# A GNN edge network on one core: first keys evicted ahead of head 3's norm, the rectifier in eight pieces inside the chain, and GpSimd adding the halves of the squared outputs

## The reference

```python
scale = 1.0 / np.sqrt(2.0 * O)
q_i = K_v[dst]
alpha = concatenate([q_i * K_v[src], q_i * K_E], axis=1) * scale
gate = sigmoid(_ln(alpha, ln_g[h], ln_b[h]))
m = concatenate([V_v[src], V_E], axis=1)
m = (m @ Wu[h] + bu[h]) * gate
m = _leaky(_ln(m @ Wm[h] + bm[h], mln_g[h], mln_b[h]))
heads.append(segment_sum(m, dst, num_segments=n))
```

## Time and profile before

| what | value |
|---|---|
| median of 3 runs | 12,400.16 us (12,395.85 to 12,402.57) |
| the profiled execution's own time | 12,403.94 us |
| its span, first to last instruction | 12,402.1 us |
| mean granted TensorE clock | 0.978 |
| busy over the span: PE, DVE, ACT, POOL | 76%, 69%, 54%, 53% |
| edge network, first to last gate (L722) | 4,182 to 10,434 us |

### The profile page before, as it was taken

One profiled execution on the slowest core, in us unless ns is written; L12 is line 12 of the kernel. 1 busy time (PEld: TensorE's weight loads), 2 busy tenths in 40 slices (PEclk: granted clock), 3 DMA queues, 4 the chain that ended last, 5 costly groups with the idle time before them and its releaser, 6 DMA issues.

```text
span 12402.1 us, 195341 instructions
## 1 busy us (share of the span) xinstructions
PE 9426.5 (76%) x48422; PEld 6119.9 (49%) x48423; DVE 8554.8 (69%) x19173; ACT 6685.0 (54%) x13488; POOL 6548.5 (53%) x4199
## 2 busy tenths in 40 slices
PE   1344444444446799999999999999999997769996
PEld 1233333333322566666666666666666665333222
DVE  4233333333311799999999999999999998047896
ACT  0111111111100488888888888888888886026442
POOL 1588888888840366666666666666666664000000
PEclk9999999999999799999999999999999998989997
DMA  9866666666678455555555555555555553869663
GB/s 412 257 163 150 152 150 151 150 152 152 149 234 337 153 152 152 152 152 152 152 152 152 152 152 152 152 152 152 152 152 152 152 152 109 355 255 358 206 218 118
DMA packets 1446102, 2253.42 MB, mean 182 GB/s; under 512 B 352561, under 2 KB 981762, under 8 KB 1432131
## 3 DMA queue, kind: packets, MB, share of 16 engines
q1 hardware_dynamic: 1129144, 1975.67, 48.0%
q0 software_dynamic: 312672, 272.36, 13.6%
q10 hardware_dynamic: 4144, 3.51, 0.1%
HBM read 1758.01 MB, written 492.97 MB: 181 GB/s over the span
## 4 chain that ended last, share of the span: by engine, by line
PE 42%; POOL 15%; ACT 15%; issue 12%; DMA 8%; DVE 3%; SPq 3%; ACTq 1%; DVEq 0%; POOLq 0%; PEldq 0%
POOL adj L1473 14%; ACT arena L1014 8%; PE psum L1274 6%; PE psum L1259 6%; PE psum L1248 5%; PE psum L1345 5%; DMA arena<-adj 5%; PE psum L1240 4%; PE psum L1214 4%; SPq L1520 3%; ACT acc L1005 3%; DMA adj<-put_val,put_idx 3%; PE psum L1390 2%; PE psum L1266 2%; ACT arena L986 2%
## 5 line engine op out<-in xcount | busy, mean ns | idle before, releaser
L1473 POOL DMA_INDIRECT adj<-put_val,put_idx x1616 | 2640.7, 1634 | 842.6 <-issue 477.2
L1155 PE MATMUL psum<-ke,arena 64*128 64x256 f32 x3232 | 1451.8, 640 | 1883.2 <-DMA arena<-in_edge_t 1883.2
L1014 ACT ACTIVATE arena<-arena 128x128 f32<-128x128 f32 x6464 | 2624.5, 501 | 19.1 <-DVE arena L788 9.1
L1434 POOL DMA_INDIRECT arena<-table,idx_blk x1616 | 1938.1, 1199 | 451.3 <-issue 409.3
L1155 PEld LDWEIGHTS psum<-ke,arena 64*128 64x128 f32 x3232 | 1041.6, 330 | 2292.9 <-issue 2025.9
L971 ACT ACTIVATE arena<-psum 128x512 f32<-128x512 f32 x808 | 482.5, 597 | 2921.5 <-PE psum L1155 2611.7
L1486 POOL TENSOR_TENSOR arena<-arena,mg 128x1024 f32<-128x1024 f32 x404 | 953.6, 2360 | 1973.7 <-DVE arena L800 1973.7
L1248 PE MATMUL psum<-arena,wvu 128*128 128x512 f32 x3232 | 1655.3, 594 | 0.0
L1259 PE MATMUL psum<-wm,arena 128*128 128x64 f32 x12928 | 1616.3, 278 | 0.0
L1259 PEld LDWEIGHTS psum<-wm,arena 128*128 128x128 f32 x12928 | 1505.4, 192 | 183.3 <-issue 181.5
L1020 ACT ACTIVATE arena<-psum,cols 128x512 f32<-128x512 f32 x1616 | 1263.2, 782 | 495.0 <-PE psum L1240 494.6
(11 more groups left out here) (218 smaller groups left out, 12787.6 us busy)
## 6 DMA issues: line engine op xcount, KB each, us to landing
arena<-adj SPq DMA_DIRECT2D x192, 1568.0 KB, 12.5
arena<-adj SPq DMA_DIRECT2D x336, 896.0 KB, 4.7
kept_keys<-arena SPq DMA_DIRECT2D x404, 512.0 KB
arena<-kept_keys SPq DMA_DIRECT2D x404, 512.0 KB
arena<-table1q SPq DMA_DIRECT2D x1616, 128.0 KB
adj<-arena SPq DMA_DIRECT2D x98, 1568.0 KB
arena<-in_edge_t SPq DMA_DIRECT2D x808, 128.0 KB
kept_hot<-arena SPq DMA_DIRECT2D x404, 256.0 KB
```

The lines of the kernel that those rows point to most:

```text
L1014: A.activation(to, at_, ACT.Identity, bias=shift[z][:, n:n + 1], scale=rstd[z][:, n:n + 1]).then_inc(normed, 1)
L1155: last = M.matmul(psum[:, 2 + 2 * z + j, t * H * D:(t + 1) * H * D], edge0[z][:, 2 * j + t, :], ke[D:P, :], start=True, stop=True)
L1434: K.indirect_dma_start(out=dst[:, t, :], out_offset=None, in_=table, in_offset=bass.IndirectOffsetOnAxis(ap=idx[:, t:t + 1], axis=0)).then ...
L1473: K.indirect_dma_start(out=adj, out_offset=bass.IndirectOffsetOnAxis(ap=put_idx[s][:, j:j + 1], axis=0), in_=put_val[s][:, j:j + 1], in_of ...
```

## The change

ScalarE empties the first bank of keys before it normalizes head 3, no longer after it. VectorE's rectifier is cut into eight pieces of 128 columns, and one follows each of eight small steps of the chain; the wait for GpSimd's offset stands ahead of the first piece and `msg_ready` is raised by the last. The squares are laid out from column 1 (column 0 holds epsilon), GpSimd adds the upper 32 to the lower 32 of each tile-head in place, in two halves of a group (`fold`), and VectorE sums 33 columns instead of 65, one step later in the chain, behind a wait for both folds. On GpSimd one fold stands between the gathers and the weighing, the other between weighing and offset, which used to follow each other directly.

```diff
         o_taken = sem("o_taken")
+        o_folded = sem("o_folded")
...
-                if now[4]:
-                    dve.wait_ge(y_affine, 2 * (i - 3))
-                    V.scalar_tensor_tensor(y[z], y[z], 0.01, y[z], ALU.mult, ALU.max).then_inc(msg_ready, 1)
...
+                piece = Q // 8
+
+                def leaky(part):
+                    if now[4]:
+                        if part == 0:
+                            dve.wait_ge(y_affine, 2 * (i - 3))
+                        own = y[z][:, part * piece:(part + 1) * piece, :]
+                        done = V.scalar_tensor_tensor(own, own, 0.01, own, ALU.mult, ALU.max)
+                        if part == 7:
+                            done.then_inc(msg_ready, 1)
...
                 if now[0]:
                     dve.wait_ge(stats1, Q * (i + 1))
-                if now[3]:
-                    dve.wait_ge(o_taken, 2 * (i - 2))
+                else:
+                    after(dve, chain1, i * CH)
...
-                small_step(V.tensor_reduce(var[:, Q:2 * Q], o_sq[odd], AX, ALU.add))
                 settle()
 
                 small_step(V.scalar_tensor_tensor(d2, d2, P / 4.0, d2, ALU.mult, ALU.mult))
+                if now[3]:
+                    dve.wait_ge(o_folded, 2 * (i - 2))
+                small_step(V.tensor_reduce(var[:, Q:2 * Q], o_sq[odd][:, :, 0:D // 2 + 1], AX, ALU.add))
                 settle()
                 small_step(V.tensor_tensor(var[:, 0:Q], d2, m2, ALU.add))
+                leaky(0)
                 settle()
                 small_step(V.tensor_scalar(root.bitcast(I32), var.bitcast(I32), -0.5, MAGIC, ALU.mult, ALU.add))
+                leaky(1)
...
                 small_step(V.tensor_tensor(u, u, var, ALU.mult))
+                leaky(7)
                 settle()
...
-                    A.activation(o_sq[z][:, pair, 0:D], ps, ACT.Square, scale=(P / D) ** 0.5)
+                    A.activation(o_sq[z][:, pair, 1:D + 1], ps, ACT.Square, scale=(P / D) ** 0.5)
...
+                if inside or i + 1 < NG:
+                    take_q(i + 1, 0)
                 if now[1]:
                     norm(i - 1, (s + 3) % U, odd, 3)
-                if inside or i + 1 < NG:
-                    take_q(i + 1, 0)
...
+            def fold(g, z, j):
+
+                pool.wait_ge(o_taken, 2 * g + j + 1)
+                own = o_sq[z][:, 2 * j * H:2 * (j + 1) * H, :]
+                low, high = own[:, :, 1:D // 2 + 1], own[:, :, D // 2 + 1:D + 1]
+                K.tensor_tensor(low, low, high, ALU.add).then_inc(o_folded, 1)
...
                 gather(pair[s][:, :, 0:ROW1], table1, idx, kv_in[s])
+                if not isinstance(g, int) or g >= 4:
+                    fold(g - 4, z, 0)
                 if not isinstance(g, int) or g >= 5:
-                    affine(g - 5, 1 - z)
+                    weigh(g - 5, 1 - z)
+                if not isinstance(g, int) or g >= 4:
+                    fold(g - 4, z, 1)
+                if not isinstance(g, int) or g >= 5:
+                    offset(g - 5, 1 - z)
```

More of the change, by code:

```diff
@@ L763, in sweep1 @@
                 small_step(V.scalar_tensor_tensor(m2, st[:, :, 2], P * EPS1, st[:, :, 5], ALU.add, ALU.add))
-                small_step(V.tensor_reduce(var[:, Q:2 * Q], o_sq[odd], AX, ALU.add))
                 settle()
                 small_step(V.scalar_tensor_tensor(d2, d2, P / 4.0, d2, ALU.mult, ALU.mult))
+                if now[3]:
+                    dve.wait_ge(o_folded, 2 * (i - 2))
+                small_step(V.tensor_reduce(var[:, Q:2 * Q], o_sq[odd][:, :, 0:D // 2 + 1], AX, ALU.add))
                 settle()
                 small_step(V.tensor_tensor(var[:, 0:Q], d2, m2, ALU.add))
+                leaky(0)
                 settle()
                 small_step(V.tensor_scalar(root.bitcast(I32), var.bitcast(I32), -0.5, MAGIC, ALU.mult, ALU.add))
+                leaky(1)
                 settle()
                 small_step(V.scalar_tensor_tensor(u, root, 1.0, root, ALU.mult, ALU.mult))
+                leaky(2)
                 settle()
                 small_step(V.tensor_tensor(u, u, var, ALU.mult))
+                leaky(3)
                 settle()
                 small_step(V.scalar_tensor_tensor(u, u, -10.0 / 3.0, u, ALU.add, ALU.mult))
+                leaky(4)
                 settle()
                 small_step(V.scalar_tensor_tensor(root, u, 5.0, root, ALU.add, ALU.mult))
+                leaky(5)
                 settle()
                 small_step(V.scalar_tensor_tensor(u, root, -0.5 * 0.375 ** 3 * P ** 0.5, root, ALU.mult, ALU.mult))
+                leaky(6)
                 settle()
                 small_step(V.tensor_tensor(u, u, var, ALU.mult))
+                leaky(7)
                 settle()
@@ L1480, in _, with weigh @@
             pool.wait_ge(dve_step, marks["sweep1"])
-            def affine(g, z):
+            def fold(g, z, j):
[3 more added lines that the diff above has]
+                K.tensor_tensor(low, low, high, ALU.add).then_inc(o_folded, 1)
+            def weigh(g, z):
                 y4 = y[z].rearrange("p (t h) d -> p t (h d)", t=G)
@@ L1487, in affine, with offset @@
                                 ALU.mult).then_inc(y_affine, 1)
+            def offset(g, z):
+                y4 = y[z].rearrange("p (t h) d -> p t (h d)", t=G)
                 pool.wait_ge(y_affine, 2 * g + 1)
@@ L1498, in sweep1 @@
                 gather(pair[s][:, :, 0:ROW1], table1, idx, kv_in[s])
+                if not isinstance(g, int) or g >= 4:
+                    fold(g - 4, z, 0)
                 if not isinstance(g, int) or g >= 5:
-                    affine(g - 5, 1 - z)
+                    weigh(g - 5, 1 - z)
[3 more added lines that the diff above has]
+                    offset(g - 5, 1 - z)
             blocks(sweep1, kv_in, idx_ready, 2)
             for g in range(NG, NG + 5):
-                affine(g - 5, (g - 5) % 2)
+                if g < NG + 4:
+                    fold(g - 4, g % 2, 0)
+                weigh(g - 5, (g - 5) % 2)
+                if g < NG + 4:
+                    fold(g - 4, g % 2, 1)
+                offset(g - 5, (g - 5) % 2)
         @block.sync
```

## The result

The changed kernel takes 12,313.53 us (median of 20 runs, 12,301.64 to 12,420.13), the one before 12,401.87 in the same rounds. The ratio is 0.9933 [0.9923, 0.9943]: faster by 0.67%, 88 us. The forecast was 12,475 and slower. The time lies inside the range, on the other side of no change. The profiled execution took 12,309.15 us, with a span of 12,307.3.

A forecast was written before the change was run, and what follows sets the result against it. Two nearly equal loops, TensorE with ScalarE and VectorE with GpSimd, take 15.52 us a group; changed, the second bounds at 15.70: 400 x (15.70 - 15.52) = +72 us, 12,475. Own range 12,350 to 12,600, widened for the second rival to 12,240 to 12,610.

The forecast's parts named there:

- TensorE's wait: Before the second expansion L1214, for ScalarE's eviction of the first keys: 0.85 us a group, to go with keys first.
- loop A: TensorE and ScalarE, edge network: 15.52 us a group before, 14.67 once the wait for the keys goes.
- head 3's norm: ScalarE, behind the keys: ends at 19.25, just in time for TensorE's transposes at 19.3.
- The read port: VectorE instructions with two SBUF inputs and GpSimd ones reading SBUF exclude each other throughout; full hold 0.62, 12,475.
- Both holds: VectorE's first chain step held 1.13 us by GpSimd's offset, its product 0.37 by fold 0.
- the rival without a hold: Long GpSimd operations let VectorE's reads through: loop B 14.17, TensorE bounds with 14.67, 12,060 us; chance 0.15.
- Loop B: VectorE and GpSimd, edge network: 15.52 us a group before, 15.67 after, 15.70 on average; bounds the changed kernel.
- held once only: Rival: fold 0 slips clear of the product or holds are shorter; loop 15.30, 12,310 us; chance 0.15.
- point of decision: Total hold on VectorE in loop B of 1.3 us: below that the kernel gets faster.
- Pieces dearer: Rival: rectifier pieces at 0.30 us each, loop 15.98, 12,585 us; chance 0.08 together with fold dearer.
- fold dearer: Rival: GpSimd's fold at 0.90 us, loop 16.0, 12,590 us; chance 0.08 together with pieces dearer.

The follow-up runs named there:

- the probes: Kernel before plus one unused 16-column VectorE step per group during GpSimd's weighing, reading two SBUF tensors or one: 12,813.52 and 12,397.39 us.
- the first probe: Kernel before plus one unused 16-column VectorE add of two SBUF tensors per group during GpSimd's weighing: 12,813.52 us (one execution).
- the sums last: Changed kernel without folds, ScalarE's `take_sums` moved behind head 3's norm and the keys, norm ahead of keys again: 12,079.83 us, 0.9744 of the kernel before.

## Why the prediction was wrong

*TensorE's wait.* Right. Its row is gone, and with the folds out a group takes 14.79 where loop A was put at 14.67. The 0.1 between them is head 3's norm: the prediction had it just in time for the transposes, and it comes 0.2 late.

*The read port.* Right, and shown by the probes. Both holds are in the changed kernel, in all but about ten of its groups, and the rival without a hold (12,060) is out.

*Loop B as the bound.* Right: with the second hold removed (fold 0 beside the gates) the period falls from 15.22 to 14.81. For the kernel before, though, the loops were not equal: the keys alone bring 0.10 a group and the pieces alone nothing, so loop A bounded and loop B stood at 15.42.

*The size of loop B.* This failed. The prediction summed 15.67; the group shown above takes 15.20 from L818 to L818. By the prediction's own terms, from the end of L818 at 7001.39:

- The offset ends at 7006.84, 5.45 later, where 5.69 stood. The fold lasts 0.75, as taken, but GpSimd's records overlap: from weighing to fold it is 2.31 from start to start (taken 2.44), from fold to offset 0.70 (taken 0.81). The handover between two long operations was carried over from the earlier trace rows and charged twice.
- The first gate begins 3.93 after that, where 4.18 stood. L769 ends at 7006.89; without the hold it takes 0.18, so it got through at about 7006.71, 0.13 ahead of the end of the offset's record (records of GpSimd are rough at just this size, but the last section has two more such cases). And a step with its piece takes 0.30 (the two L751 shown start at 7008.03 and 7008.32, 0.29 apart), so a piece occupies 0.20, the lower bound that was given, and not 0.215.
- Two gates 1.32, where 1.40 stood. The rest of it was waiting: with the keys alone they take 1.33.
- The product is held 0.49, where 0.37 stood: fold 0 starts 1.18 after the first gate, where 1.03 was reckoned, and the product is there earlier.
- Product, hot rows and scaling 4.01, where 4.03 stood.

Together -0.24 - 0.25 - 0.08 + 0.12 - 0.02 = -0.47. Instead of 0.15 over the period of before (0.18 on average) the group shown is 0.32 under it, and the median one, at 15.22, 0.30. Over the 385 groups counted that is 116 us faster; about 29 us of it are lost again in groups at the lower clock, which leaves 87 of the 88 measured.

So the step that failed is the sum of loop B, in its terms for GpSimd's two operations with the fold between, for the chain, and for the gates. The mechanism, the two holds on loop B, stood. The difference that decided the sign, 0.18 us a group, was a difference of two sums of over 15 us with a dozen terms each, most of them read from one group to 0.01 and carried over with their handovers; an error of 0.03 in each, all on one side, turns it. The measured time is almost that of the rival "held once only", 12,310, but that rival is not what happened: the product is held in nearly every group. That the time fell so near to it is luck. The prediction's point of decision, a total hold of 1.3 us, is off by the same terms: 1.0 and 0.49 give 1.5, and the kernel is faster.

*Pieces dearer, fold dearer.* Neither came: a piece takes 0.20, the lower bound, and a fold 0.75, about what was taken (0.74).

## What to carry to other kernels

Before work goes to GpSimd, list what VectorE executes beside it: here an instruction with two SBUF inputs and a long GpSimd one that reads SBUF ran one after the other, and the held one looks busy in every table. Moved by a microsecond to where VectorE reads one SBUF tensor, the same addition cost 189 us less. Count also what the added GpSimd work delays behind it: here that used up all it saved VectorE. Where two loops are within a few per cent of each other, judge parts of a change in pairs: keys and pieces were worth 0.3% and nothing singly, and 2.3% together. And when a forecast is the small difference of two long sums, take terms from start to start over the whole sequence, and let the chances say that the sign is open.

## What was not expected of the hardware

**The hold begins ahead of the fold's record.** With fold 0 between the gathers, L804 starts at 6659.10 and is held to 6660.23, the fold's record runs from 6659.43 to 6660.17. The step is stopped 0.33 us before the record of what stops it begins. Ahead of the fold GpSimd's third gather runs, to 6659.41. The gather alone does not explain it: in the changed kernel chain steps pass beside the third gather unheld (L801 at 7010.07, 0.18 us, gather from 7009.54 for 1.14). What holds in these 0.33 us stays open. At the other end the release comes ahead of the record's end each time: about 0.13 in the chain beside the offset, 0.11 for the product beside fold 0 (7012.09 + 0.49 against 7012.69), and about 0.16 in the first probe (its step would take some 0.18 by itself, and ends 0.02 after the record). So a hold is not exactly the overlap of two records.

**Spells at the lower clock.** Between 4,414 and 10,289 us of the changed kernel the granted clock falls ten times to about 0.5, the level of 1.2 GHz, for some 7 us. One of them, three stretches (columns as above), and TensorE's rows there:

```profile
7283.00:7287.00 4.00, 3.54 (x21) 2.04 (x19) 3.96 (x15) 4.00 (x10) 3.11 (x4) 1.00 0.85 273
7287.00:7294.00 7.00, 7.00 (x30) 5.79 (x29) 5.19 (x11) 2.97 (x6) 3.29 (x3) 0.51 0.62 172
7294.00:7298.00 4.00, 4.00 (x27) 2.96 (x26) 3.82 (x15) 3.42 (x9) 3.56 (x3) 1.00 0.04 8
```

```profile
7284.72 1.15 PE L1292 MATMUL psum<-arena 128*128 128x128 f32 x8 [0.46 <-issue]
...
7286.12 2.87 PE L1277 MATMUL psum<-wm,arena 128*128 128x64 f32 x16
7288.79 2.02 PE L1292 MATMUL psum<-arena 128*128 128x128 f32 x8
```

The last eight matmuls take 2.02 instead of 1.11 us. Ahead of the fall TensorE had waited 0.46. In the group behind the spell neither VectorE step is held (the shortest values of L769 and L700 above are such). Each spell costs one group of 16.3 and one of 16.6 to 18.0, about 3 us over both, 29 for the ten; that is the difference between the mean period of 15.30 and the undisturbed 15.22. In the second profile of the same kernel there are 14 of them at other places, and the one execution of 12,420 had a mean clock of 0.929 where the others had 0.974 to 0.976. Fold 0 between the gathers has 96, at 95.8% busy TensorE. The kernel before (94.9% busy, with a wait of 0.78 in each group) has none in the same part. Up to their last groups neither have the versions with the keys alone, the pieces alone, the folds alone, without the folds (99.6%), with fold 0 beside the gates (99.5%) or with the sums last (98.8%). The changed kernel is 97.0% busy. So neither more nor less waiting of TensorE on average goes with it. What sets it off stays open.
